# A GNN kernel: nodes laid out by partition in the prologue, small steps moved to ScalarE, and another tail and unread products at the layer borders

## The chip, the cores and the metric

The kernel runs on one core of a Trainium2 chip. The metric is the device time of one execution in microseconds (us), the median of three runs. The core has five engines with queues of their own: TensorE (PE; its weight loads are PEld), VectorE (DVE), ScalarE (ACT), GpSimd (POOL) and SyncE (SP), which here only issues DMAs. The profile comes from one further execution, recorded by the hardware profiler.

## The reference

6250 nodes of 128 features and 200,000 edges (`src`, `dst`), sorted by `dst`. A graph attention layer (GAT) with four heads comes first, then three message passing (MP) layers with batch norm between them, then a final linear map; a residual and a layer norm follow both parts.

```python
xh = (x @ W).reshape(-1, H, C); xi = xh[dst]; xj = xh[src]
alpha = leaky_relu((xi * a_i).sum(-1) + (xj * a_j).sum(-1), 0.2)
...                                   # softmax of alpha over the edges of each dst
x1 = layernorm(x + segment_sum(xj * alpha, dst))
for l in range(3):
    h = emb if l == 0 else (h - mu) * rsqrt(var + EPS) * gamma[l-1] + beta[l-1]
    hk = relu(concat(h[dst], h[src]) @ linA_w[l].T + linA_b[l])
    w = sigmoid(hk @ linB_w[l].T + linB_b[l])
    prop = segment_sum(w * h[src], dst)
    emb = relu(concat(h, prop) @ lin_w[l].T + lin_b[l])
return layernorm(x1 + emb @ final_w.T + final_b)
```

## The kernel before

Edges are worked on in groups of 512 (`GE`), 4 tiles (`T`) of 128 in the partitions: 391 groups in each of four stages, one for GAT and one for each MP layer. A stage first writes a table of one row of 256 floats per node to HBM (`T0`, seen as gat_rows, for GAT; `T1`, mp_rows, for MP). GpSimd's `gather` then fetches the rows of `src` with four indirect DMAs per group into the ring `G` of eight slots, and TensorE, VectorE and ScalarE turn each group into sums for a window of 32 `dst` nodes, added into `acc`. Each engine's program is written out by hand, and semaphores alone order them. GpSimd's first gather of a stage waits until every store of that stage's table has landed.

**Prologue.** `dst` and `src` are loaded as rows of 2048 edges in 98 partitions (`dstI`, `srcI`), 96 full rows first and the tails after; `dst_loaded` counts three DMAs, the last of them issued behind the src rows. SyncE issues these, W0, the two attention columns (`acol`) and the MP weights; ScalarE issues x in five loads. VectorE's instructions up to the index columns are chained by the semaphore `prep` (`then`), and the `PREP_...` numbers say how many must be done: constants, `PREP_REL` (offset of each dst in its window, `relF`), `PREP_REL16` (the same in bf16, `rel16`), `PREP_SRC`, `PREP_MORE` (counts of extra windows), `PREP_IDX`. `edge_columns` on TensorE transposes `relF` and `srcF` with 16 products each, and VectorE copies the result from PSUM to `rel_all` and `idx_all`. GpSimd clears `acc` and `mh` once `PREP_MORE` is reached.

T0 is made in 17 steps `j` of three blocks of 128 nodes. For each, TensorE transposes x (`table_turn`) and multiplies (`table_gat`), ScalarE copies the transposed x (`table_x`), and the result is copied by ScalarE (`table_rows`) or, for j = 6, 7, 9, 10, 12, 13, 15, 16, by VectorE, behind its index columns. SyncE stores each (`store_table`); the ring `tbl` has four slots, so step j waits for the store of step j - 4. The scores of dst (`si_all`, seen as pen) go to `SI` (gat_si) in three stores.

**Border of two layers.** The last group of a layer is followed by steps in which only later stages of the last groups run (`step` with `off >= stop`); `mp_order` gives VectorE's order of stages: `mp_hidden` (pen), `mp_logit` (junk), `mp_C` (selw) and `mp_E` (acc). `mp_agg` on TensorE, for one group, waits for selw of this group and for `mp_E` of the group two before, whose PSUM bank it reuses. Then ScalarE makes the 13 pieces of ReLU (`l_emb`), VectorE the statistics of 25 pieces, and `scaled`, the weights times the new scale. TensorE makes the 25 pairs of table blocks from `scaled`, VectorE adds `constB`, SyncE stores. `extra_windows` handles groups whose nodes span more than one window; each engine reads two numbers from `windows` for it, and skips its body if there are none.

## Time and profile before

| | us |
|---|---|
| median of three runs | 8181.65 |
| lowest, highest | 8179.83, 8184.32 |
| profiled execution, its own time | 8189.58 |
| its span | 8187.5 |
| GpSimd busy | 5969.7 (73%) |
| VectorE busy | 4897.3 (60%) |
| TensorE busy | 4800.6 (59%) |
| ScalarE busy | 1347.8 (16%) |

The span counts from the first to the last recorded instruction. Busy time leaves out the issue of DMAs by SyncE and ScalarE and register work. "Idle before" of a group is the time its engine stood still just before it, with what ended that. A row with a queue's name, such as SPq or ACTq, is an instruction of the engine's sequencer.

### The profile page before, as it was taken

The numbers are of one execution on the slowest core, as the hardware profiler recorded it, in microseconds if no ns is written. First come the engines' busy times: TensorE is split into PE (matmuls) and PEld (weight loads), VectorE is DVE, ScalarE is ACT, GpSimd is POOL, SyncE is SP. The second block draws the span as 40 slices with busy tenths as digits, with TensorE's granted clock in tenths as the row PEclk, the third lists the DMA queues.
The fourth block names the chain that finished last, engine by engine and source line by source line (L and its number), as shares of the span: only waits on it lengthen the run. The fifth ranks groups of instructions, "written<-read, shape, count | busy, mean of one in ns | idle before, by whom it ended". The sixth has DMA issues, their size and how long they took to land.

```text
span 8187.5 us, 133929 instructions
## 1 busy us (share of the span) xinstructions
PE 4800.6 (59%) x26657; PEld 4100.9 (50%) x26658; DVE 4897.3 (60%) x25933; ACT 1347.8 (16%) x5213; POOL 5969.7 (73%) x6318
## 2 busy tenths in 40 slices
PE   5888888888744444445564444445446544444545
PEld 5777777777544444444454444444445444444444
DVE  6778778777655555555565555555555555555555
ACT  2333333333300000000020000000011000000002
POOL 5777777777477777777757777777766777777775
PEclk6555555555655555555565555555556555555555
DMA  5444444444444444444454444444435444444443
GB/s 155 131 134 131 131 131 132 132 131 124 135 129 131 129 129 129 131 129 129 129 155 129 131 129 129 129 131 129 129 113 170 129 131 129 129 129 131 129 129 104
DMA packets 613022, 1074.04 MB, mean 131 GB/s; under 512 B 305928, under 2 KB 371368, under 8 KB 612428
## 3 DMA queue, kind: packets, MB, share of 16 engines
q0 software_dynamic: 300288, 820.39, 34.9%
q1 hardware_dynamic: 306076, 247.79, 10.3%
q10 hardware_dynamic: 6356, 3.20, 0.2%
q14 instruction: 279, 2.29, 0.1%
q8 instruction: 23, 0.38, 0.0%
HBM read 1025.37 MB, written 45.47 MB: 131 GB/s over the span
## 4 chain that ended last, share of the span: by engine, by line
POOL 46%; issue 22%; PE 14%; DMA 7%; DVE 7%; DVEq 2%; POOLq 1%; ACT 1%; ACTq 0%
POOL G L740 46%; DMA G<-mp_rows,idx 5%; PE ps L1717 5%; PE ps L1817 3%; DMA G<-gat_rows,idx 2%; PE ps L1679 2%; DVE junk L1509 2%; PE ps L1714 1%; PE ps L1706 1%; DVEq L1117 1%; PE ps L1769 0%; PE ps L1770 0%; DVE selw L1518 0%; POOLq L737 0%; POOLq L736 0%
## 5 line engine op out<-in xcount | busy, mean ns | idle before, releaser
L740 POOL DMA_INDIRECT G<-mp_rows,idx x4692 | 4439.0, 946 | 1564.2 <-issue 1384.5
L1817 PE MATMUL ps<-selw,G 128*128 128x32 f32 x9384 | 2216.7, 400 | 587.6 <-DVE selw L1518 579.3
L1817 PEld LDWEIGHTS ps<-selw,G 128*128 128x128 f32 x9384 | 2088.9, 328 | 868.9 <-issue 760.0
L1498 DVE TENSOR_TENSOR pen<-ps,G 128x512 f32<-128x512 f32 x1173 | 811.3, 692 | 2730.1 <-DMA G<-mp_rows,idx 2726.9
L1807 PE MATMUL ps<-awin,ring 96*128 96x128 bf16 x4692 | 713.4, 307 | 2315.5 <-DVE ring L1483 2312.4
L740 POOL DMA_INDIRECT G<-gat_rows,idx x1564 | 1489.7, 952 | 497.9 <-issue 442.6
L1807 PEld LDWEIGHTS ps<-awin,ring 96*128 96x128 bf16 x4692 | 408.9, 132 | 2467.4 <-DVE ring L1483 2463.4
L963 ACT ACTIVATE gate<-logit,params 128x4 f32<-128x4 f32 x1173 | 348.6, 297 | 5327.0 <-DVE junk L1509 5205.2
L1509 DVE SCALAR_TENSOR_TENSOR junk<-pen,ps 128x128 f32<-128x128 f32 x4692 | 1056.3, 278 | 0.1
L1483 DVE TENSOR_TENSOR ring<-ring,ps 96x512 bf16<-96x512 bf16 x1173 | 793.3, 676 | 37.1 <-DMA ring<-rel_dst 37.1
L1717 PE MATMUL ps<-sel,weighted 128*128 128x32 f32 x3128 | 748.9, 404 | 0.0
L1717 PEld LDWEIGHTS ps<-sel,weighted 128*128 128x128 f32 x3128 | 696.2, 327 | 25.2
L1679 PE MATMUL ps<-ident,G 128*128 128x128 f32 x1564 | 428.0, 429 | 171.9 <-DMA G<-gat_rows,idx 170.7
L851 ACT ACTIVATE pen<-ring,negbig 128x512 f32<-128x512 bf16 x391 | 282.1, 721 | 1165.8 <-DVE ring L1129 1157.0
L1155 DVE CUSTOM_DVE_ANT_0 junk<-ps,pen 128x512 f32<-128x512 f32 x391 | 268.2, 686 | 264.6 <-issue 257.2
L1679 PEld LDWEIGHTS ps<-ident,G 128*128 128x128 f32 x1564 | 280.1, 217 | 186.7 <-issue 129.2
L1509 DVE DVE_READ_ACCUMULATOR junk<-pen,ps 128x1 f32 x4692 | 369.4, 79 | 0.0
L1706 PE MATMUL ps<-sel,ex 128*4 128x32 f32 x3128 | 230.4, 238 | 199.2 <-DVE tt L1280 199.2
L1488 DVE TENSOR_TENSOR ps<-ps,rel_all 128x128 f32<-128x128 f32 x1173 | 333.0, 284 | 0.0
L1518 DVE TENSOR_TENSOR selw<-ps,gate 128x128 f32<-128x128 f32 x1173 | 331.1, 282 | 0.2
L1706 PEld LDWEIGHTS ps<-sel,ex 128*4 128x4 f32 x3128 | 161.6, 105 | 330.4 <-issue 245.2
L833 ACT COPY idx<-idx_all 128x4 int32 (+1 forms) x1568 | 283.5, 182 | 23.4 <-issue 11.3
(202 smaller groups left out, 4682.6 us busy)
## 6 DMA issues: line engine op xcount, KB each, us to landing
ring<-rel_dst SPq DMA_DIRECT2D x294, 384.0 KB
G<-mp_rows,idx POOLq DMA_INDIRECT x4692
ring<-rel_dst SPq DMA_DIRECT2D x98, 512.0 KB
awin<-mp_dst_rows SPq DMA_DIRECT2D x1173, 24.0 KB
G<-gat_rows,idx POOLq DMA_INDIRECT x1564
mp_rows<-acc SPq DMA_DIRECT2D x36, 512.0 KB, 3.0
mp_dst_rows<-acc SPq DMA_DIRECT2D x36, 384.0 KB, 5.0
sm<-gat_si SPq DMA_DIRECT2D x391, 0.5 KB
```

The source lines that it names most:

```text
L740: pool.indirect_dma_start(out=G[:, u, width * t:width * (t + 1)], out_offset=None, in_=table, in_offset=bass.IndirectOffsetOnAxis(ap=idx[: ...
L963: nc.scalar.activation(gate[:, off % 4, :], logit[:, off % 4, :], ACT.Sigmoid, bias=params[:, l, C_BB:C_BB + 1]).then_inc(done["gate"], 1)
L1483: v.tensor_tensor(selT16[0:S * W, off % 4, :], relbc16[0:S * W, off % U, :], nodeP[0:S * W, :].to_broadcast([S * W, GE]), ALU.is_equal).th ...
L1488: v.tensor_tensor(selP[:, off % 4, :].rearrange("p (t n) -> p t n", t=T), iotaP.unsqueeze(1).to_broadcast([P, T, W]), rel4, ALU.is_equal). ...
L1498: v.tensor_tensor(pen[:, off % 2, :].rearrange("p (t c) -> p t c", t=T), PS[off % 2][:, :].rearrange("p (t c) -> p t c", t=T), Grows[:, of ...
L1509: v.scalar_tensor_tensor(junk[:, P * t:P * t + P], pen[:, off % 2, P * t:P * t + P], 0.0, wP, ALU.max, ALU.mult, accum_out=logit[:, off % ...
L1518: v.tensor_tensor(selw[:, off % 4, :].rearrange("p (t n) -> p t n", t=T), one.rearrange("p (t n) -> p t n", t=T), gate[:, off % 4, :].unsq ...
L1679: i = tr(PS[off % 2][:, P * t:P * t + P], Grows[:, off % U, t, D:2 * D], ident[:, :])
L1706: i = mm(PS[4 + b][0:H, 2 * W:3 * W], ex4[:, b, H * t:H * t + H], sel[:, off % U, W * t:W * t + W], start=(t == 0), stop=(t == T - 1))
L1717: i = mm(PS[4 + b][:, 0:W], R[:, b, D * t:D * t + D], sel[:, off % U, W * t:W * t + W], start=(t == 0), stop=(t == T - 1))
L1807: i = mm(PS[off % 2][:, D * t:D * t + D], selT16[0:S * W, off % 4, P * t:P * t + P], awin[:, off % 4, :], start=True, stop=True)
L1817: i = mm(PS[2 + off % 2][:, 0:W], Grows[:, off % U, t, 0:D], selw[:, off % 4, W * t:W * t + W], start=(t == 0), stop=(t == T - 1))
```

## The change

1. Prologue, layout: blocks of the first 48 hold the nodes 48p + b in partition p instead of 128b + p (`by_partition`). x is loaded, and T0 and SI are stored, with that order in mind, so that a partition's nodes stand together in HBM: a load of x has 128 pieces of 5 KB where it had 1280 of 512 bytes, a store of T0 128 pieces of 3 KB where it had 384 of 1 KB, a store of SI 128 pieces of 384 bytes where it had 2304 of 16. The rows of T0 stand where they stood.
2. W0 and the attention columns are issued before dst and src. VectorE makes all its constants before it waits for them.
3. `rel16` is made by ScalarE, as a plain cast, after table step 3, and waits there for `PREP_REL`; the copy that wraps `idx_all` around is ScalarE's too.
4. Four table stores (`REL_AT`) instead of three stand before the stores of the offsets, and SI is stored at steps 8, 16 and 17.
5. VectorE reads the numbers for `extra_windows` ahead of each stage's loop instead of behind it.
6. Tail of an MP layer: VectorE's order in the last steps is `mp_last`.
7. Ahead of the table of layers 1 and 2, TensorE makes eight products of 512 columns into a PSUM bank that nothing reads.

VectorE in the prologue, from the dst offsets to the first table copies. Here xT holds the two lists and relF, and ring is the table's ring. Before:

```order
L1062 TENSOR_TENSOR xT<-xT,baseF 98x2048
L1065 TENSOR_SCALAR G<-xT 98x4x128x4
L1069 CAST xT<-xT 98x2048
L1073 SCALAR_TENSOR_TENSOR xT<-xT 2x704
L1074 TENSOR_REDUCE moreF<-xT 98x4
L1075 TENSOR_TENSOR moreF<-moreF,baseF 98x4
L1076 TENSOR_SCALAR moreI<-moreF 98x4
L1077 TENSOR_SCALAR moreI<-moreI 98x4
L1083 COPY rel_all<-ps 128x4x98 x4
L1083 CAST idx_all<-ps 128x4x98 x4
L1085 COPY idx_all<-idx_all 128x16
```

and after:

```order
L1076 TENSOR_TENSOR xT<-xT,baseF 98x2048
L1080 CAST xT<-xT 98x2048
L1084 SCALAR_TENSOR_TENSOR xT<-xT 2x704
L1085 TENSOR_REDUCE moreF<-xT 98x4
L1086 TENSOR_TENSOR moreF<-moreF,baseF 98x4
L1087 TENSOR_SCALAR moreI<-moreF 98x4
L1088 TENSOR_SCALAR moreI<-moreI 98x4
L1094 COPY rel_all<-ps 128x4x98 x4
L1094 CAST idx_all<-ps 128x4x98 x4
L1102 COPY ring<-ps 128x3x128
```

The step that writes G (rel16) and the copy from idx_all to idx_all are gone; the rest stands as it stood.

ScalarE in the prologue, from the end of table step 3 to step 6 (G is rel16 here, pen the scores). Before:

```order
L811 COPY ring<-ps 128x384
L817 COPY ring<-ps 128x3x128
L819 COPY ring<-ps 128x3x128
L820 COPY pen<-ps 128x12
L811 COPY ring<-ps 128x384
L817 COPY ring<-ps 128x3x128
L819 COPY ring<-ps 128x3x128
L820 COPY pen<-ps 128x12
L811 COPY ring<-ps 128x384
L817 COPY ring<-ps 128x3x128
```

and after:

```order
L819 COPY ring<-ps 128x384
L825 COPY ring<-ps 128x3x128
L827 COPY ring<-ps 128x3x128
L828 COPY pen<-ps 128x12
L840 CAST G<-xT 98x4x128x4
L819 COPY ring<-ps 128x384
L825 COPY ring<-ps 128x3x128
L827 COPY ring<-ps 128x3x128
L828 COPY pen<-ps 128x12
L819 COPY ring<-ps 128x384
L825 COPY ring<-ps 128x3x128
```

The cast stands behind step 3's copies and ahead of everything that ScalarE does for steps 4 and 5.

VectorE at the end of layer 0, in its last steps (ps is PSUM, pen and junk the hidden values and logits). Before:

```order
L1498 TENSOR_TENSOR pen<-ps,G 128x512
L1529 ISA
L1529 TENSOR_TENSOR acc<-acc,ps 128x32
L1509 SCALAR_TENSOR_TENSOR junk,logit<-pen,ps 128x128 x4
L1518 TENSOR_TENSOR selw<-ps,gate 128x128
L1529 ISA
L1529 TENSOR_TENSOR acc<-acc,ps 128x32
L1518 TENSOR_TENSOR selw<-ps,gate 128x128
L1529 ISA
L1529 TENSOR_TENSOR acc<-acc,ps 128x32
L1529 ISA
L1529 TENSOR_TENSOR acc<-acc,ps 128x32
```

and after:

```order
L1530 TENSOR_TENSOR selw<-ps,gate 128x128
L1509 REGISTER_ALU
L1510 TENSOR_TENSOR pen<-ps,G 128x512
L1521 SCALAR_TENSOR_TENSOR junk,logit<-pen,ps 128x128 x4
L1541 ISA
L1541 TENSOR_TENSOR acc<-acc,ps 128x32
L1530 TENSOR_TENSOR selw<-ps,gate 128x128
L1541 ISA
L1541 TENSOR_TENSOR acc<-acc,ps 128x32
L1541 ISA
L1541 TENSOR_TENSOR acc<-acc,ps 128x32
L1541 ISA
```

The weights (selw) of the last but one group moved ahead of the last group's pen, the first addition to acc moved behind its logits; behind the last of the four additions stood two loads from windows, which now stand ahead of the loop.

The diff, cut to its core:

```diff
@@ prologue, SyncE @@
+            sp.dma_start(rhs0[:, 0:D], W0).then_inc(w0_loaded, 16)
+            with nc.allow_non_contiguous_dma(reason="columns of small weights"):
+                for ij, lo in ((0, C), (1, 0)):
+                    sp.dma_start(acol[:, ij:ij + 1], ...).then_inc(w0_loaded, 16)
             for tile, lst, loaded in edges:
                 sp.dma_start(tile[0:QS, :], ...).then_inc(loaded, 16)
-                if lst is dst:
-                    sp.dma_start(rhs0[:, 0:D], W0).then_inc(w0_loaded, 16)
...
+        def by_partition(table, lo, n):
+            return table[0:NF * NB, :].rearrange("(p b) c -> p b c", b=NF)[:, lo:lo + n, :]
...
-                sp.dma_start(T0[lo * NB:(lo + n) * NB, :].rearrange("(b n) c -> n b c", n=NB),
-                             tbl[:, j % 4, 0:n, :]).then_inc(tbl_out[j % 4], 16)
+                if lo < NF:
+                    to = by_partition(T0, lo, n)
+                else:
+                    to = T0[lo * NB:(lo + n) * NB, :].rearrange("(b n) c -> n b c", n=NB)
+                sp.dma_start(to, tbl[:, j % 4, 0:n, :]).then_inc(tbl_out[j % 4], 16)
...
-            for j in range(3):
+            for j in range(REL_AT):
                 store_table(j)
...
-            sp.wait_ge(prep, PREP_REL16)
+            sp.wait_ge(rel16_made, 1)
@@ prologue, ScalarE @@
-                act.dma_start(xall[0:NB, lo:hi, :], x[lo * NB:hi * NB, :]
-                              .rearrange("(b p) c -> p b c", p=NB)).then_inc(x_in[n], 16)
+                act.dma_start(xall[:, lo:hi, :], by_partition(x, lo, hi - lo)).then_inc(x_in[n], 16)
...
+                if j == REL_AT:
+                    act.wait_ge(prep, PREP_REL)
+                    nc.scalar.copy(rel16..., relF...).then_inc(rel16_made, 1)
...
+            nc.scalar.copy(idx_all[:, NG * T:(NG + LOOKAHEAD) * T], idx_all[:, 0:LOOKAHEAD * T]).then_inc(idx_around, 1)
@@ layers, VectorE @@
                 km = kl + windows_before(dve, l)
+                counts = windows_before(dve, l + 1), windows_before(dve, 1)
...
+                mp_last = ((2, mp_C), (1, mp_hidden), (1, mp_logit), (4, mp_E))
+
                 def step(k0, off, stop=U):
-                    for lag, stage in mp_order:
+                    for lag, stage in mp_order if off < stop else mp_last:
@@ layers, TensorE @@
                 if l > 0:
+                    pe.wait_ge(l_emb, NEM * (l - 1) + 4)
+                    for n in range(8):
+                        mm(PS[5][:, :], ident[:, :], params[:, 0, C_LP:C_LP + 4 * D], start=True, stop=True)
                     pe.wait_ge(l_w, 2 * l - 1)
```

## Rows read from the trace of the kernel before

**Rows 1.** Page, costliest groups: busy us, mean ns of one | idle before, releaser.

```profile
L740 POOL DMA_INDIRECT G<-mp_rows,idx x4692 | 4439.0, 946 | 1564.2 <-issue 1384.5
```

**Rows 2.** GpSimd's waits, whole span: us in total, times, longest us.

```profile
POOL G L740 <- DMA mp_rows<-acc: 135.5, 3, 50.1
```

**Rows 3.** Chain of waits, 0 to 100 us: start us, us, what.

```profile
14.53 5.17 ACTq L797
23.45 0.28 ACT WT L804
...
59.28 7.10 DMA gat_rows<-ring
...
67.27 2.32 DMA gat_rows<-ring
...
70.48 1.10 POOL G L740
```

**Rows 4.** Timeline, all engines, 0 to 60 us: start us, us, engine, line.

```profile
0.79 0.40 SPq L530 DMA_DIRECT2D xT<-in_dst  x1
...
12.66 0.23 DVE L1038 TENSOR_SCALAR ablk<-dhc,acol 128x4 f32<-128x4 f32 x1 [9.46 <-DMA acol<-in_L_gnn_att]
...
15.71 1.23 DVE L1057 CAST xT<-xT 98x2048 f32<-98x2048 int32 x1
...
22.03 5.37 DVE L1065 TENSOR_SCALAR G<-xT 98x2048 bf16<-98x2048 f32 x1
...
31.81 0.27 ACT L820 COPY pen<-ps 128x12 f32<-128x12 f32 x1
...
32.54 3.47 DVE L1083 COPY rel_all<-ps 128x392 f32<-128x392 f32 x4
...
32.63 10.78 POOL L730 MEMSET acc<- 128x12800 f32 x1 [29.58 <-DVE moreI L1077]
...
36.92 3.45 DVE L1083 CAST idx_all<-ps 128x392 int32<-128x392 f32 x4 [0.91 <-PE ps L1644]
...
40.41 8.40 DVE L1085 COPY idx_all<-idx_all 128x16 int32<-128x16 int32 x1
...
43.34 5.44 POOL L731 MEMSET mh<- 128x6400 f32 x1
...
48.84 0.56 DVE L1092 COPY ring<-ps 128x384 f32<-128x384 f32 x1
```

**Rows 5.** DMA issues, 0 to 100 us: KB each, median us to landing.

```profile
gat_rows<-ring SPq DMA_DIRECT2D x16, 384.0 KB, 3.5
...
gat_si<-pen SPq DMA_DIRECT2D x2, 36.0 KB, 7.7
```

**Rows 6.** DMA queues, 10 to 11 us (q1 SyncE, q10 ScalarE): packets, MB, share.

```profile
q1 hardware_dynamic: 44, 0.22, 97.7%
q10 hardware_dynamic: 43, 0.02, 13.7%
```

**Rows 7.** DMA packets in sum, 2 to 15 us.

```profile
DMA packets 3429, 3.18 MB, mean 245 GB/s; under 512 B 345, under 2 KB 3244, under 8 KB 3246
```

**Rows 8.** Timeline, border of layers 0 and 1, 4116 to 4133 us.

```profile
4116.14 3.59 PE L1817 MATMUL ps<-selw,G 128*128 128x32 f32 x16 [1.61 <-DVE acc L1529]
...
4120.19 7.73 ACT L991 ACTIVATE mh<-acc,params 128x500 f32<-128x500 f32 x13 [4.07 <-DVE acc L1529]
4121.73 8.10 DVE L1568 BATCH_NORM_STATS2 stats<-mh 128x6 f32<-128x250 f32 x25 [1.68 <-ACT mh L991]
...
4131.97 1.22 PE L1769 MATMUL ps<-scaled,mh 128*128 128x256 f32 x2 [12.23 <-DVE scaled L1441]
```

**Rows 9.** Stretches there: us, each engine's busy (x), TensorE clock, DMA share, GB/s.

```profile
4131.90:4137.60 5.70, 5.63 (x17) 4.90 (x18) 2.09 (x10) 0.00 (x0) 0.00 (x0) 0.50 0.00 0
4137.60:4158.00 20.40, 20.40 (x97) 17.97 (x96) 16.14 (x24) 0.00 (x0) 0.00 (x0) 0.99 0.83 280
```

**Rows 10.** One line (windows_before), VectorE's queue: ns min/median/max.

```profile
L499 DVEq TENSOR_LOAD <-windows x12: 297/309/328, 2057.1 to 8132.7; - x12
```

More of the change, by code:

```diff
@@ L43 @@
 PREP_IDENT = 3
-PREP_ABLK = PREP_IDENT + 6
-PREP_CONST = PREP_ABLK + 13
-PREP_REL = PREP_CONST + 5
-PREP_REL16 = PREP_REL + 1
-PREP_SRC = PREP_REL16 + 1
+PREP_CONST = PREP_IDENT + 17
+PREP_ABLK = PREP_CONST + 2
+PREP_REL = PREP_ABLK + 5
+PREP_SRC = PREP_REL + 1
 PREP_MORE = PREP_SRC + 5
-PREP_IDX = PREP_MORE + 2 * T + 1
+PREP_IDX = PREP_MORE + 2 * T
 def reached(k0, off, n, done=None):
@@ L119, in gnn_kernel @@
     TO = D + 2 * H
-    SIB = (6, 12, NTB)
+    SIB = (8, 16, NTB)
+    REL_AT, SRC_AT = 4, 7
     TW = 2 * D
@@ L501, in extra_windows @@
         @contextmanager
-        def extra_windows(eng, q):
-            before = windows_before(eng, q)
-            total = windows_before(eng, 1)
+        def extra_windows(eng, q, counts=None):
+            before, total = counts or (windows_before(eng, q), windows_before(eng, 1))
             with eng.If(total > 0):
@@ L530, in _ @@
                 sp.dma_start(tile[0:QS, :], lst[0:QS * QW].rearrange("(q e) -> q e", e=QW)).then_inc(loaded, 16)
-                if lst is dst:
-                    sp.dma_start(rhs0[:, 0:D], W0).then_inc(w0_loaded, 16)
-                    with nc.allow_non_contiguous_dma(reason="columns of small weights"):
-                        for ij, lo in ((0, C), (1, 0)):
-                            sp.dma_start(acol[:, ij:ij + 1], att[0, :, lo:lo + C].rearrange(
-                                "h (c o) -> h c o", o=1)).then_inc(w0_loaded, 16)
             sp.wait_ge(pads_filled, 3)
@@ L829, in _ @@
                     table_rows(j - 1)
+                if j == REL_AT:
+                    act.wait_ge(prep, PREP_REL)
+                    nc.scalar.copy(rel16.rearrange("q (c t p) -> q c p t", c=CQ, t=T),
+                                   relF.rearrange("q (c p t) -> q c p t", c=CQ, t=T)).then_inc(rel16_made, 1)
             def copy_idx(k0, off):
@@ L1036, in _ @@
             then(v.memset(epsc[:, :], EPS))
-            dve.wait_ge(w0_loaded, 48)
-            then(v.tensor_scalar(ablk[:, 0:H], dhc[:, :], acol[:, 0:1], None, ALU.mult))
-            then(v.tensor_scalar(ablk[:, H:2 * H], dhc[:, :], acol[:, 1:2], None, ALU.mult))
-            assert done[0] == PREP_ABLK
             then(v.memset(negbig[:, :], -BIG))
@@ L1054, in _ @@
             assert done[0] == PREP_CONST
+            dve.wait_ge(w0_loaded, 48)
+            then(v.tensor_scalar(ablk[:, 0:H], dhc[:, :], acol[:, 0:1], None, ALU.mult))
+            then(v.tensor_scalar(ablk[:, H:2 * H], dhc[:, :], acol[:, 1:2], None, ALU.mult))
+            assert done[0] == PREP_ABLK
             dve.wait_ge(dst_loaded, 48)
@@ L1064, in _ @@
             assert done[0] == PREP_REL
-            then(v.tensor_single_scalar(rel16.rearrange("q (c t p) -> q c p t", c=CQ, t=T),
-                                        relF.rearrange("q (c p t) -> q c p t", c=CQ, t=T), NONE16, ALU.min))
-            assert done[0] == PREP_REL16
             dve.wait_ge(src_loaded, 48)
@@ L1084, in _ @@
                                        PS[4 + t][:, :].rearrange("p (c q) -> p c q", c=CQ)[:, :, 0:QP]))
-            then(v.tensor_copy(idx_all[:, NG * T:(NG + LOOKAHEAD) * T], idx_all[:, 0:LOOKAHEAD * T]))
             assert done[0] == PREP_IDX
@@ L1302, in _ @@
             dve.wait_ge(acc_cleared, 2)
+            counts = windows_before(dve, 0), windows_before(dve, 1)
             load_bases(0, 0, U)
@@ L1338, in added @@
                 dve.wait_ge(x_scan, scan[0])
-            total = windows_before(dve, 1)
+            total = counts[1]
             with dve.If(total > 0):
@@ L1353, in _ @@
             dve.sem_inc(x_free, 1)
-            with extra_windows(dve, 0) as at:
+            with extra_windows(dve, 0, counts) as at:
                 now, k0 = one_by_one(gat_sems, at.w), GR + at.n
@@ L1553, in _ @@
                 dve.sem_inc(x_free, 1)
-                with extra_windows(dve, l + 1) as at:
+                with extra_windows(dve, l + 1, counts) as at:
                     now, k0 = one_by_one(mp_sems, at.w), GR + at.n
@@ L1657, in _ @@
                 table_gat(j - 1)
-                if j in (4, 7):
-                    edge_columns((4, 7).index(j))
+                if j in (REL_AT, SRC_AT):
+                    edge_columns((REL_AT, SRC_AT).index(j))
             pe.wait_ge(wraw_loaded, 48)
```

17 lines of the change are left out of this document (12 added, 5 removed).

## The prediction, made before the changed kernel was run

> **What bounds the kernel now.** I began with the page's costliest groups: GpSimd issues the indirect gathers, 0.95 us each with 0.3 us of issue between them [rows 1], one every 1.25 us. There are 6256 (four for each of 391 groups, in four stages), so 6256 x 1.25 = 7820 of 8187.5 us is this pace, and the change leaves its instructions alone. What can move is the time in which GpSimd has no gather to issue: the prologue, 70.48 us to the first gather [rows 3], and the borders between stages, three waits for the table of the next layer, 135.5 us in all, 50 for each of the last two [rows 2]. So the views to read are the chain of waits and the timeline of the prologue, the DMA view there, and the timeline and clock of one border.
>
> In the prologue the chain [rows 3] runs: ScalarE issues the loads of x and is stuck in that until 22.1 us (the 14.53 piece is the last of five); then, through TensorE and the table copies, to VectorE's index columns, which end at 40.4; then one copy of 16 columns from SBUF to SBUF that lasts 8.4 us, until GpSimd's second memset ends at 48.78 [rows 4]; then tables 6 to 16, in which the last waits until 66.41 for a store; then that last store and the first gather.
>
> **Prologue, step by step.** The new head of the chain is the arrival of the dst list, call it D, since the column work starts from it. In the old profile VectorE reached it at 15.71, just after its constants [rows 4], so it had landed by then. In the new one it lands later. The x loads now are pieces of 5 KB instead of 512 B, and the weights stand first in SyncE's queue. The two queues take turns packet by packet: at 10 to 11 us 44 against 43 packets, although one kind was 8 KB and the other 512 B [rows 6]. So when x's packets are ten times as large, x gets its bytes early and the list late. Per DMA engine SyncE's queue has 24 small weight packets (384 over 16 engines) and then 12 of 8 KB (both lists; the dst tail waits behind the src list), against 40 of x. By D nearly all of x, 36/40 of 3.2 MB, and 1.6 MB of lists and weights have passed: 4.5 MB. The old start moved 245 GB/s between 2 and 15 us [rows 7], a border with large pieces 280 [rows 9]: D = 2 + 4.5/0.245 = 20.4 or 2 + 4.5/0.28 = 18.1. I take 18.5, since the pieces are large, with 15.7 (what the old order reached) and 20.4 as bounds.
>
> The DMA page of the Trainium skill (DMA: Bandwidth & Descriptors, Queues, rings and completion order) says that an engine drains a whole packet, typically 9 to 17 descriptors, of one queue before it switches. Taken as turns of so many x pieces, all of x would pass ahead of the weights and the lists come last, D = 2 + 4.8/0.28 = 19.1, 0.6 us more; the counts of 44 and 43 speak for turns of one piece.
>
> From D, all on VectorE [rows 4]: cast, minimum, base and difference, 22.03 - 15.71 = 6.32. The bf16 step of 5.37 goes to ScalarE. Then src cast, pads, maximum and counts, 32.54 - 27.4 = 5.1. Then four copies for rel_all, 3.47, and four for idx_all, 3.45. The copy of 16 columns goes to ScalarE. Sum D + 18.35 = 36.9 against 48.84: 11.9 us. Of this, 5.37 + 8.43 + about 0.9 of waiting for TensorE is removed, and 2.8 is given back by the later D.
>
> What runs beside: the weights land at about 10 (24 packets per engine in turns with x of 0.24 us, 2 + 7, and the completion), against 12.66 [rows 4], and ScalarE, whose seven x issues should now cost about 0.4 us each like SyncE's of 96 pieces [rows 4], is free by then. Tables 0 to 3 took 8.6 us from the weight copy at 23.45 [rows 3] to 32.08 [rows 4], so they end near 19. Then ScalarE waits for the differences at D + 6.3 = 24.8 and casts. Behind this wait stand its copies for tables 4, 5 and 6, and TensorE, which waits for the same event. The cast isn't in the trace. Bounds: four times ScalarE's 0.59 for 500 columns [rows 8], 2.4, and VectorE's 5.37 with the same scattered write. I take 2.4. TensorE then is at the src columns at 24.8 + 2.4 + three tables of 1.3 = 31, when VectorE has just made the first rel_all copy (30.8). So the cast is covered by the src half of VectorE's work; at 5.37 about 0.2 us shows, and without cover 3.
>
> Tables 6 to 16: from 48.84 table 12 was stored at 59.28 [rows 3], 10.4 later, and then the store took 7.1, since it queued with a store of gat_si in pieces of 16 bytes (7.7 us to landing, against 3.5 for table rows [rows 5]). Those pieces are now 384 bytes. Table 16 can be copied at 10.4 + 3.5 = 13.9, ends 0.86 later, lands 2.3 later [rows 3], and the gather starts 0.86 after: 18.0, with the store's own issue 18.3, against 70.48 - 48.84 = 21.6. First gather at 36.9 + 18.3 = 55.2: **15.3 us earlier**. Bounds of this part: 2.5 less if TensorE keeps its pace (it idles 2 us now, not 10), 2 more if the copies run slower beside the memset, which now ends near 46. rel_all's copies ran beside it at 0.87 us for 392 columns, against 0.56 for 384 afterwards [rows 4].
>
> **Borders.** The eight unread products start when four of the 13 ReLU pieces are done, 4120.19 + 4 x 0.59 = 4122.6 [rows 8]. TensorE was idle until 4131.97 and then worked 5.7 us at a granted 0.5 (the 1.2 GHz level) before it rose to 0.99 (2.4 GHz) [rows 9]. At the high level the 97 instructions of 20.4 us give 0.21 each, four to a pair of blocks, 0.84; an unread product of 512 columns costs the same, and 1.68 at the low level. With the same 5.7 us at the low level, 3.4 products are done, the other 4.6 take 3.9, end 4132.2. The true products so start 0.2 later but all at the high level, which saves 5.7/2 = 2.85: 2.65 a border, **5.3 us for two**. Behind them are queued only the table's products, and VectorE and the stores follow these (rate 280 GB/s with the clock high, which the stores kept up with). Bounds: 3 above; below, the eight never raise the clock, 8 x 1.68 = 13.4, a loss of 4.1 each.
>
> The tail order: the two last products of a layer took 3.59 together, 1.8 each [rows 8]. The new order lets the weights of the last but one group be made early, but its product also needs its PSUM bank, and that is free only after the addition of two groups before, which the new order puts behind the last group's logits. So not 1.8 but about 0.15 a layer comes out, for the addition of 0.18 that no longer stands ahead of the logits: **0.4 us for three**. Bounds 0 and 5.4.
>
> The register loads: two of 0.31 [rows 10] with their 0.2 of register work, about 1 us, leave the spot between the last addition and the statistics (VectorE's 1.68 idle at 4121.73, of which some 0.6 is ReLU [rows 8]). They stand at the top of the next layer now, where 0.5 us of them shows ahead of the scaling. All of this ends before 4132.2, when the unread products let TensorE go, so I cost it at nothing; without that cover it would be a gain of 0.4 a border.
>
> Sum: 15.3 + 5.3 + 0.4 = 21.0 us. The profiled span of 8187.5 becomes 8166.5, and the median of 8181.65 becomes 8160.6 by the same difference; the run around the profile took 8189.58.
>
> **Rivals.** *Copies locked by the memset.* The 8.4 us copy shows that GpSimd's memset can hold VectorE for its whole length. If the table copies are held as well, table 6 waits for D + 11.4 + 16.15 = 46.1 instead of 36.9: 9.2 us lost, 8169.8. Against it: rel_all's copies, from PSUM too, ran in the same memset [rows 4]. *ScalarE still stuck.* If the loads' issue doesn't shrink, tables 0 to 3 end at 32 as before, the cast at 34.5, the src columns at 38 and the indices at 41.5: 8165.2. Its cause was 1280 pieces a load, against some 128 now. *The clock doesn't rise for unread products:* 5.3 not gained and 2 x 4.1 lost, 8174.1. Against it: the old rise came after the same kind of steady work. *The list comes late.* This is the one that ends slower. x's large packets sit between the list's, and every us of D costs one us, since VectorE has nothing else to do; from D = 18.5 + 21.0 = 39.5 on the whole is slower, 8182 and up. It needs 4.5 MB at 120 GB/s, half of the lowest long mean seen. Up to D = 25 it gives 8167.
>
> **How the numbers follow.** Forecast with its bounds 0.72 (8153 to 8169), locked copies 0.07, stuck issue 0.06, clock 0.07, late list 0.08, of which 0.03 is beyond the point of no gain. Range 8153 to 8173: it leaves out part of the clock case, the late list and the far ends. A measurement of this kernel can tell 0.2%, 16.4 us, that is 8165.3: about four fifths of the forecast lie below it, 0.59. Slower than 8198 needs D near 56; I leave 0.02 for it and what I don't see. Within 0.2%: 0.39.
>
> **What would show it.** The dst cast starts at 17 to 20 and not at 15.7; ScalarE's weight copy at about 10; the cast on ScalarE takes 2 to 3 us; table 6's first copy at 37, right after the index copies; the first gather at 55. At a border, eight products from 4122.6 (shifted), a granted clock near 1 for the whole table, and a wait of GpSimd of 47 instead of 50 us. Wrong would be: D above 21, a long piece among VectorE's copies while GpSimd's memset runs, TensorE not done with the unread products when the scaling is, or another pace than 1.25 us per gather.

## The result, and the profile after

| us | before | after |
|---|---|---|
| median | 8179.64 (15 runs) | 8164.16 (15 runs) |
| lowest, highest | 8176.54, 8184.32 | 8161.66, 8167.09 |
| span of the profiled execution | 8187.5 | 8162.0 |

The ratio is 0.9981, with a 95% interval of 0.9973 to 0.9988: 15.5 us or 0.19% faster, a hair inside the 0.2% that I had named as the limit of what can be told. The forecast was 8160.6 in 8153 to 8173; the sum of 21.0 us was 5.5 too large. The total hides 2 us of that, by luck: the forecast started from 8181.65, the median of three runs, and over 15 runs it is 8179.64.

The two spans differ by 25.5 us, 10 more than the medians: the profiled execution of before took 8189.58 us, more than any of its 15 runs, and that of after 8163.91, close to its median. The starts of GpSimd's first and last gather of each stage divide them:

| piece, us | before | after | difference |
|---|---|---|---|
| start to first gather | 70.48 | 61.20 | -9.3 |
| attention stage, first to last gather | 1964.9 | 1958.0 | -6.9 |
| its last gather to layer 0's first | 120.4 | 120.2 | -0.2 |
| three MP stages, first to last gather | 5864.8 | 5861.9 | -2.9 |
| border of layers 0 and 1 | 50.9 | 48.4 | -2.5 |
| border of layers 1 and 2 | 51.0 | 47.8 | -3.3 |
| last gather to the end | 64.9 | 64.6 | -0.3 |

Without the stages themselves the pieces give 15.6 us, the difference of the medians. What the stages add (9.8 us) is for the most part in the length of the gathers (6.7 and 2.5 us of busy time); these are GpSimd's costliest groups by form (busy us, mean ns of one), of before and of after:

```profile
L740 POOL DMA_INDIRECT G<-gat_rows,idx x1564 | 1489.7, 952 | 497.9 <-issue 442.6 <-DMA gat_rows<-ring 21.7 <-DVE weighted L1265 19.8
```

```profile
L749 POOL DMA_INDIRECT G<-gat_rows,idx x1564 | 1483.0, 948 | 489.3 <-issue 461.3 <-ACT idx L845 14.8 <-DVE weighted L1275 13.1
```

**Prologue.** The timeline of after, 0 to 62 us (start us, us, engine, line, what; in brackets the idle time before it and what ended it), which answers to [rows 4]; the line numbers are higher now:

```profile
0.78 2.77 ACTq L806 DMA_DIRECT2D G<-in_x  x5
...
15.59 0.23 DVE L1066 TENSOR_SCALAR ablk<-dhc,acol 128x4 f32<-128x4 f32 x1 [9.87 <-DMA acol<-in_L_gnn_att]
...
20.23 1.23 DVE L1071 CAST xT<-xT 98x2048 f32<-98x2048 int32 x1 [4.15 <-DMA xT<-in_dst]
...
26.55 9.40 ACT L840 CAST G<-xT 98x2048 bf16<-98x2048 f32 x1 [1.39 <-DVE xT L1076]
...
31.66 3.42 DVE L1094 COPY rel_all<-ps 128x392 f32<-128x392 f32 x4
...
31.75 10.77 POOL L739 MEMSET acc<- 128x12800 f32 x1 [28.70 <-DVE moreI L1088]
...
36.32 1.73 PE L1648 MATMUL ps<-rhs,ring 128*128 128x136 f32 x6 [6.23 <-ACT ring L819]
...
39.55 2.05 PE L1658 MATMUL ps<-ident,xT 98*128 98x98 f32 x16
...
40.27 3.46 DVE L1094 CAST idx_all<-ps 128x392 int32<-128x392 f32 x4 [5.19 <-PE ps L1658]
...
43.76 0.56 DVE L1102 COPY ring<-ps 128x384 f32<-128x384 f32 x1
...
61.20 1.10 POOL L749 DMA_INDIRECT G<-gat_rows,idx  x1 [13.30 <-ACT idx L845]
```

ScalarE's issue of x no longer blocks it. The cast on ScalarE takes 9.40 us. Behind it stand the copies for table steps 4 to 6; TensorE waits 6.23 us for one of them and reaches the src list at 39.55, and VectorE waits 5.19 us for that. VectorE's work on either side of this wait took what it took before.

How the list comes in, by the stretches of after (us, five engines' busy time, TensorE clock, DMA share, GB/s), then the DMA queues of after (q1 SyncE, q10 ScalarE: packets, MB, share) in the same 18.2 us, and last those in the final 2.2 us of them:

```profile
2.00:20.20 18.20, 4.25 (x19) 4.08 (x20) 3.43 (x20) 3.13 (x7) 0.99 (x2) 1.00 1.01 288
```

```profile
q10 hardware_dynamic: 849, 3.19, 55.7%
q1 hardware_dynamic: 1023, 2.06, 45.4%
```

```profile
DMA packets 454, 0.51 MB, mean 234 GB/s; under 512 B 46, under 2 KB 424, under 8 KB 444
...
q1 hardware_dynamic: 328, 0.40, 84.8%
q10 hardware_dynamic: 126, 0.11, 22.5%
```

At 288 GB/s, 18.2 us are 5.2 MB: all of x (3.2 MB) and 2.06 MB of SyncE's queue. The small packets at the end, on SyncE's queue, are not of a list (those are of 8 KB): what stands behind the lists in that queue are the MP weights. The lists are 1.6 MB and W0 0.07, so 0.4 MB of them had passed by 20.2.

**Border.** The timeline of layers 0 and 1 in after, 4098 to 4143 us, which answers to [rows 8]:

```profile
4102.47 0.19 DVE L1541 TENSOR_TENSOR acc<-acc,ps 128x32 f32 x1 [1.52 <-PE ps L1834]
4102.80 7.73 ACT L1005 ACTIVATE mh<-acc,params 128x500 f32<-128x500 f32 x13 [3.91 <-DVE acc L1541]
4103.55 8.10 DVE L1582 BATCH_NORM_STATS2 stats<-mh 128x6 f32<-128x250 f32 x25 [0.88 <-ACT mh L1005]
...
4105.37 10.08 PE L1781 MATMUL ps<-params,ident 128*128 128x512 f32 x16 [3.03 <-ACT mh L1005]
...
4114.13 0.16 DVE L1449 RECIPROCAL mv<-mv 128x1 f32<-128x1 f32 x1 [1.51 <-issue]
...
4115.29 0.60 PE L1786 MATMUL ps<-scaled,mh 128*128 128x256 f32 x2
...
4142.31 0.94 POOL L749 DMA_INDIRECT G<-mp_rows,idx  x1 [47.50 <-DMA mp_rows<-acc]
```

and the stretches there, which answer to [rows 9]:

```profile
4105.37:4111.40 6.03, 6.03 (x7) 2.52 (x8) 6.03 (x20) 6.01 (x10) 0.00 (x0) 0.51 0.00 0
4111.40:4115.50 4.10, 4.10 (x11) 1.90 (x10) 2.31 (x9) 1.21 (x6) 0.00 (x0) 1.00 0.01 2
4115.50:4135.90 20.40, 20.40 (x100) 18.09 (x99) 15.62 (x26) 0.00 (x0) 0.00 (x0) 1.00 0.72 242
```

The clock rises 6 us after the unread products begin, and the whole table runs at 2.4 GHz.

### The profile page after: what moved, and what is told of

The parts are those of the page before. It is cut to its first block, busy times and chain, and to the rows that moved or that the text cites. A ratio compares the mean times of both kernels' runs of the same rounds, so it can differ in the third digit from the quotient of the medians.

```text
span 8162.0 us, 133990 instructions
## 1 busy us (share of the span) xinstructions
PE 4842.2 (59%) x26689; PEld 4118.1 (50%) x26690; DVE 4894.9 (60%) x25931; ACT 1352.9 (17%) x5215; POOL 5960.5 (73%) x6318
## 4 chain that ended last, share of the span: by engine, by line
POOL 54%; issue 22%; PE 8%; DMA 7%; DVE 6%; DVEq 1%; POOLq 1%; ACT 0%; SPq 0%; ACTq 0%
POOL G L749 54%; DMA G<-mp_rows,idx 5%; PE ps L1834 3%; DMA G<-gat_rows,idx 2%; DVE junk L1521 2%; PE ps L1731 1%; PE ps L1693 1%; DVEq L1127 1%; DVE weighted L1275 0%; PE ps L1786 0%; POOLq L746 0%; PE ps L1787 0%; DVE selw L1530 0%; PE ps L1728 0%; POOLq L745 0%
## 5 line engine op out<-in xcount | busy, mean ns | idle before, releaser
L845 ACT COPY idx<-idx_all 128x4 int32 (+1 forms) x1568 | 283.4, 182 | 23.5 <-issue 11.3
L1216 DVE TENSOR_REDUCE e<-ps 128x32 f32<-128x96 f32 x391 | 100.5, 257 | 299.1 <-PE ps L1709 298.7
L1275 DVE TENSOR_TENSOR weighted<-G,ps 128x512 f32<-128x512 f32 x391 | 268.8, 687 | 0.0
```

The source lines that it names most:

```text
L845: nc.scalar.copy(idx[:, T * (off % U):T * (off % U) + T], idx_all[:, bass.ds(k0 * T + off * T, T)]).then_inc(idx_ready, 1)
```

## Experiments

All but before_again start from the changed kernel. They ran in four sets, each on one chip and with its own runs of the kernel before. In two of the sets (rel16_on_vector, cast_written_in_order, no_unread_products and old_tail_order; before_again, prologue_three_edits and all_edits) the kernel before itself took 10555 and 10389 us, since GpSimd stood still for about 3 us again and again inside the stages, whatever the kernel; so of these the prologue and the pieces of a border are compared, event against event. This wait of GpSimd in before_again (us in total, times, longest us) has no counterpart in the first records, and what caused it is not known:

```profile
POOL G L740 <- remote: 968.2, 348, 3.6
```

### The prologue: the cast

**rel16_on_vector**: VectorE makes the bf16 copy again.

```diff
+            then(v.tensor_single_scalar(rel16.rearrange("q (c t p) -> q c p t", c=CQ, t=T),
+                                        relF.rearrange("q (c p t) -> q c p t", c=CQ, t=T), 255.0, ALU.min))
-                if j == REL_AT:
-                    act.wait_ge(prep, PREP_REL)
-                    nc.scalar.copy(rel16..., relF...).then_inc(rel16_made, 1)
```

> The changed kernel with one step undone: the bf16 copy of the offsets is made by VectorE again, behind the differences, as before. The changed kernel's median is 8164.2, its first gather at 61.2. My theory after seeing its trace: the cast took ScalarE 9.40 us and held TensorE's transposes of the src list behind it, so handing it over brought almost nothing. Then VectorE's own chain sets the end: 20.2 + 6.3 + 5.4 + 5.1 + 3.5 + 3.5 = 44.0 for table step 6 against 43.8, first gather at 61.4, total 8164. Rival (the forecast's sum): moving it was worth 5.4 us, the lateness of table step 6 has another cause (the later arrival of the list alone), and undoing it costs 5.4: table step 6 at 49, first gather at 66.6, total 8169.6.

Its timeline (its median is 10499.6, against 10494.6 to 10499.0 of the other three of its set):

```profile
20.47 1.23 DVE L1068 CAST xT<-xT 98x2048 f32<-98x2048 int32 x1 [4.43 <-DMA xT<-in_dst]
...
26.79 5.58 DVE L1076 TENSOR_SCALAR G<-xT 98x2048 bf16<-98x2048 f32 x1
...
44.42 0.56 DVE L1102 COPY ring<-ps 128x384 f32<-128x384 f32 x1
...
61.60 1.10 POOL L750 DMA_INDIRECT G<-gat_rows,idx  x1 [7.86 <-ACT idx L842]
```

The first gather is at 61.6, 41.1 us after the list; with the cast on ScalarE it is 41.0 in the first record (61.20 - 20.23), and 41.0 and 40.2 in two kernels of this set with the same prologue (no_unread_products, old_tail_order). So handing the cast over brought nothing: the rival's 5.4 us are refuted.

**cast_written_in_order**: the same elements, walked in the order in which they are written.

```diff
-                    nc.scalar.copy(rel16.rearrange("q (c t p) -> q c p t", c=CQ, t=T),
-                                   relF.rearrange("q (c p t) -> q c p t", c=CQ, t=T))
+                    nc.scalar.copy(rel16.rearrange("q (c t p) -> q c t p", c=CQ, t=T),
+                                   relF.rearrange("q (c p t) -> q c t p", c=CQ, t=T))
```

> The changed kernel with ScalarE's cast walking its elements in another order: the same 2048 per partition, written one behind the other in bf16 and read with a stride of 16 bytes, where the changed kernel reads in order and writes with a stride of 256 bytes. Theory: the scattered 2-byte write is what makes 9.40 us; written in order the cast takes 2.4 us (four times 0.59 for 500 columns), it is covered, table step 6 starts 5.1 us earlier at 38.7, the first gather at 56.1, total 8159.1. Rival: the cast is slow for its size or its type or for either stride, it stays above 5 us, and the total stays within 1 us of 8164.

```profile
20.90 1.23 DVE L1071 CAST xT<-xT 98x2048 f32<-98x2048 int32 x1 [4.98 <-DMA xT<-in_dst]
...
27.22 4.01 ACT L840 CAST G<-xT 98x2048 bf16<-98x2048 f32 x1 [2.35 <-DVE xT L1076]
...
35.84 3.43 DVE L1094 CAST idx_all<-ps 128x392 int32<-128x392 f32 x4
...
39.31 0.56 DVE L1102 COPY ring<-ps 128x384 f32<-128x384 f32 x1
...
56.73 1.10 POOL L749 DMA_INDIRECT G<-gat_rows,idx  x1 [8.17 <-ACT idx L845]
```

The cast takes 4.01 us instead of 9.40: the scattered write cost more than half. 2.4 was still too low, but at 4.0 VectorE waits for nothing (no idle time before idx_all), and table step 6 follows the list by 18.4 us instead of 23.5, which is the forecast's own 18.35. This is the 5.1 us that the forecast missed. The totals are 10494.6 against 10499.0 and 10495.9 of the two with the slow cast in that set, too close to show 5 us.

### The prologue: the list and the layout

**dst_list_first**: SyncE issues the 96 rows of dst ahead of W0 and the attention columns, as before. **dst_tail_early**: the last two pieces of dst go ahead of the src rows.

```diff
             for tile, lst, loaded in edges:
                 sp.dma_start(tile[0:QS, :], ...).then_inc(loaded, 16)
-            sp.wait_ge(pads_filled, 3)
-            for tile, lst, loaded in edges:
+                sp.wait_ge(pads_filled, 3)
                 sp.dma_start(tile[QS:QF, :], ...).then_inc(loaded, 16)
```

> The changed kernel with SyncE's order undone: the 96 full rows of dst are issued ahead of W0 and the attention columns, as before. The dst list lands at 20.2 in the changed kernel, 15.7 or earlier before. Theory 1 (the queue's order makes it late: 384 small weight packets go ahead, each taking a turn against a 5 KB packet of x): VectorE starts its dst cast 2 to 4 us earlier, the cast of the differences, table step 6 and the first gather with it, while the weight copy comes later than 16.1. Theory 2 (the forecast's sum of bytes: what counts is all that passes until the last list packet, whatever the order within SyncE's queue, since the dst tail stands behind the src rows anyway): the start stays within 0.6 us of 20.2 and the first gather within 0.6 of the changed kernel's.

> The changed kernel with the two last pieces of dst issued right behind its 96 full rows, ahead of the src rows (behind them in the changed kernel). Theory: the dst cast waits for the tail, which waits for the src rows, six packets of 8 KB per DMA engine in turns with x; without them ahead it starts about 0.75 MB / 250 GB/s = 3 us earlier, at 17.2 instead of 20.2, and the first gather comes 3 us earlier. Rival: the full rows of dst themselves land last, or the wait for the pads holds SyncE: under 1 us.

The dst cast and the first gather, of the one and of the other:

```profile
20.49 1.23 DVE L1072 CAST xT<-xT 98x2048 f32<-98x2048 int32 x1 [2.55 <-DMA xT<-in_dst]
...
61.18 1.10 POOL L750 DMA_INDIRECT G<-gat_rows,idx  x1 [13.03 <-ACT idx L846]
```

```profile
18.16 1.23 DVE L1070 CAST xT<-xT 98x2048 f32<-98x2048 int32 x1 [2.39 <-DMA xT<-in_dst]
...
58.64 1.10 POOL L748 DMA_INDIRECT G<-gat_rows,idx  x1 [12.82 <-ACT idx L844]
```

The place of the weights in the queue changes nothing (20.5 against 20.2; tail_add_first, of the same set and with the changed kernel's prologue, has 20.5 too): what counts is all that passes until the list's last packet. The tail's place does matter: 2.1 us at the list and 2.6 at the gather against the first record, 2.4 and 3.0 against tail_add_first, where 3 was expected. Records with the same prologue put the list at 20.2 to 21.5, so differences under 1 us say nothing. The medians were 8166.65 and 8163.26, both against 8180.72 of before.

**layout_as_before**: x, T0 and SI with the old pieces (part 1 of the change undone; SI is still stored at steps 8, 16 and 17, part 4).

> The changed kernel with the node layout of before in the first 48 blocks (x loaded in pieces of 512 bytes, T0 stored in pieces of 1 KB, the scores in pieces of 16 bytes). Theory: ScalarE is stuck in issuing x until about 22 and ends table step 3 at about 32, then casts until 41.5, then copies for table steps 4 to 6: TensorE is at the src list at about 45, VectorE's columns end at 50, and the stores of the scores take 7.7 us instead of 3.5: first gather at 70 to 74, total 8173 to 8177. The other parts of the change alone would so bring nearly nothing in the prologue. Rival: the layout's share is small, since the cast bounds the prologue: first gather at 63, total 8166.

```profile
0.78 17.76 ACTq L803 DMA_DIRECT2D G<-in_x  x5
...
16.60 1.23 DVE L1069 CAST xT<-xT 98x2048 f32<-98x2048 int32 x1 [6.84 <-DMA xT<-in_dst]
...
50.34 0.56 DVE L1100 COPY ring<-ps 128x384 f32<-128x384 f32 x1
...
79.45 1.10 POOL L746 DMA_INDIRECT G<-gat_rows,idx  x1 [35.19 <-DMA gat_rows<-ring]
```

8184.44 us against 8180.72 of before in the same runs, ratio 1.0006 (0.9996 to 1.0015). The list lands 3.6 us earlier, and the first gather is 18.3 us later than in the changed kernel, 9 later than before: ScalarE is late from the issue, and the 9.40 us follow that. Both expectations were too small. The chain to table step 6 was as expected (50); the rest is behind it, 29.1 us from there to the gather against 17.4 with the new layout and 21.6 before [rows 3, 4]. Its chain of waits there (start us, us, what):

```profile
53.63 7.96 DMA gat_rows<-ring
...
68.51 10.05 DMA gat_rows<-ring
```

The last store of the table lands 10.05 us after its issue where before it took 2.32 [rows 3]. That is 7.7 us, the whole of 29.1 - 21.6. It is issued right behind the store of SI of step 16, which before stood at step 12, and of the 4032 packets from 68 to 79 us 3392 are under 512 bytes. So the loss comes from the old 16-byte pieces together with the new places of SI's stores, and this experiment prices the layout in that company, not by itself. Without the new layout the other prologue parts, with the 9.40 us cast among them, lose.

### The borders

**no_unread_products** leaves out the loop of eight products; **old_tail_order** uses `mp_order` in the last steps too.

> The changed kernel without the eight unread products ahead of the tables of layers 1 and 2. Theory: the table then starts with 5.7 us at the low clock and GpSimd's wait at each border grows by 2.65 to 3 us: 50.2 and 50.0 instead of 47.5 and 46.8, total 8169.5 to 8170. Rival: the gain at the borders came from the tail order and the moved register loads, and the products bring under 1 us each: total within 2 us of 8164.

> The changed kernel with the order of VectorE's stages in a layer's last steps as before. Theory: 0.15 to 0.2 us a layer, so from a layer's last gather to its last addition 9.0 us instead of 8.8, total 8164.7. Rival: what the order aims at, 1.8 us a layer, total 8169.6.

GpSimd's waits (us in total, times, longest us), of the one and of the other:

```profile
POOL G L749 <- DMA mp_rows<-acc: 147.2, 3, 57.5
```

```profile
POOL G L749 <- DMA mp_rows<-acc: 141.7, 3, 54.9
```

From the first true product to the next gather it takes 29.7 and 30.6 us without the unread products, 27.1 and 27.1 with them (here, and in the first record of after: 27.0 and 27.1). So they bring 2.6 and 3.5 us, 3.0 on average, where 2.85 was forecast. From the start of the last gather to the end of a layer's last addition the old order takes 16.4, 13.0 and 16.5 us, the new one 16.6, 13.1 and 16.5 in cast_written_in_order: nothing of 1.8 us, as expected, and no gain of 0.15 to 0.2 either. (The 13 to 17 instead of 9 us belong to this set.)

**tail_add_first**:

```diff
-                mp_last = ((2, mp_C), (1, mp_hidden), (1, mp_logit), (4, mp_E))
+                mp_last = ((4, mp_E), (2, mp_C), (1, mp_hidden), (1, mp_logit))
```

> The changed kernel with another order of VectorE's last steps in a layer: the addition of four groups before stands first, then the weights, hidden values and logits. Theory (the forecast's): the early weights of the last group but one gain nothing in the changed kernel since its product also waits for its PSUM bank, which the addition placed behind the last logits frees. With the addition first, that product starts 2.8 us earlier (at about 4095.9 instead of 4098.72), one of the two products that follow the last logits is gone, and a layer's last addition comes 1.5 to 1.7 us earlier: 7.2 us behind the last gather instead of 8.8, 4.8 us in all. Rival: the products wait for something else (the gate of the last group, the rows), and the last addition stays within 0.2 us.

Measured from the last gather, the last addition ends at 7.70, 7.68 and 7.85 us in the three layers, against 8.80, 8.75 and 8.92: 1.1 us a layer, not 1.6. The bank was what the early weights waited for; the weights of the last group remain. Of 3.3 us the median shows some 2 (8162.94 against 8180.72 of before: 17.8 us, where the changed kernel had 15.5; the intervals of the two ratios overlap, so the medians alone don't show it), in part since the border of layers 1 and 2 gained only 0.4: there the unread products ended 0.9 us after the scaled weights were ready. They took 8.5 to 10.2 us in the records, as the clock rose sooner or later in them.

### The kernel before once more

**before_again** is the kernel before, with nothing changed.

> The kernel before, unchanged, recorded once more. In its first record the stage of the attention layer took 1964.9 us from first to last gather, 6.9 more than in the record of the changed kernel, with 132 gathers of over 966 ns where the changed kernel and three variants of it had 66 to 69. Theory 1: that is chance of the one record (the medians differ by 15.5 us, and prologue and borders alone give 9.3 + 6.0): this record has some 67 long gathers, a stage of 1958 to 1960 us at 946 ns a gather (1964 at 949), and again 70.5 us to the first gather and borders of 50.9 and 51.0. Theory 2: the change also made this stage faster: again about 130 long gathers and 5 us more at the same length of a gather.

It had 7 long gathers and not 67 or 130, in a set where gathers are held anyway: neither theory gave that (the variants of the changed kernel had 42 to 59 in the sets with held gathers). The prologue repeats (list at 15.83, the copy of 16 columns 8.45 us, first gather 71.1).

### Edits together

**prologue_three_edits**: the cast in order, the dst tail early, and

```diff
             for n in range(BU):
                 lo, hi = n * NT, min((n + 1) * NT, NF)
+                if n == 2:
+                    act.wait_ge(dst_loaded, 48)
                 act.dma_start(xall[:, lo:hi, :], by_partition(x, lo, hi - lo)).then_inc(x_in[n], 16)
```

**all_edits** adds at the borders tail_add_first, `l_emb` + 1 and `range(7)` for the unread products, and VectorE's reads of `windows` behind the table. **all_edits_cast_behind** also puts the cast at `SRC_AT` instead of `REL_AT`, and SyncE's store of rel16 behind table store 6.

> The changed kernel with three edits in the prologue: ScalarE's cast written in order (4.0 us instead of 9.4 in an earlier run), the tail of dst ahead of the src rows (2.3 us earlier in another), and ScalarE issues the last three of its five loads of x only once the dst list has landed. Theory: the list is late because 5.2 MB pass before it at 288 GB/s; with 1.9 MB of x held back it lands at about 2 + (5.2 - 1.9 - 0.75) / 0.288 = 11 us, table step 6 follows 18.4 us later unless ScalarE's tables 0 to 3 and its cast are now last (they would put it at about 31), and the first gather comes 17.4 later, at 48 to 49: 12.5 us earlier than 61.2, total 8151.5. Rival 1: the held loads of x come back as a wait of table steps 6 and later, 21 us or more after they are issued: first gather at 54, total 8157. Rival 2: the list's own 8 KB packets bound its landing, D stays above 16: first gather at 53 or later.

> The three edits of the prologue together with three at the borders: the addition first in VectorE's last steps of a layer (1.1 us a layer in an earlier run), the register loads behind the table instead of ahead of the scaling, and seven unread products that start after the first ReLU piece instead of eight after the fourth. Theory: the scaled weights are ready 1.1 + 1.2 us earlier, at 18.7 us behind the last gather instead of 21.0 and 20.6, and the unread products have ended by then, since they start 1.8 us earlier against the ReLU: next gather at 45.8 instead of 48.4 and 47.8, and 1.1 at the end of the last layer, so 5.7 us less than the prologue's edits alone: 8146. Rival: with the earlier start the clock falls again before the table or rises no earlier, and the table starts at the low clock: at least one border no better than 47.8.

> The six edits together, and ScalarE's cast now behind its copies for table steps 4 to 6 instead of ahead of them, with SyncE's store of its result behind those tables' stores. Theory: in the run before, TensorE could not start on the src list until 29.59 (behind the cast of 4.1 us and the copies it held up), while VectorE had been ready at 26.4; with the cast behind, the index columns follow rel_all's copies at 26.4, table step 6 starts at 29.9 instead of 33.8 and the first gather at 47.3 instead of 51.2. Against the changed kernel's median of 8164.2 that is 61.2 - 47.3 = 13.9 in the prologue, 2 x 2.3 at the borders and 1.1 at the end: 8144 to 8145. Rival 1: the cast is then in the way of the copies for steps 8 and later: first gather at 51 again, total 8148. Rival 2: TensorE's table steps 4 to 6 wait for stores or x pieces: gather above 52, total over 8149.

The list is there at 11.46 in prologue_three_edits, as the sum of bytes gives, and a wait of VectorE for TensorE takes a part of it back (5.58 us before idx_all), as in all_edits (3.93). Its first gather at 54.0 is the number of rival 1, but not by that mechanism: ScalarE, which waits for the list itself before it issues the last loads, is held in that until 12.7 and makes its weight copy only at 15.15, though TensorE had the product for it at 7.9. The first row below shows the same in the last kernel. Its prologue:

```profile
0.78 12.17 ACTq L807 DMA_DIRECT2D G<-in_x  x5
...
11.72 1.23 DVE L1072 CAST xT<-xT 98x2048 f32<-98x2048 int32 x1 [3.20 <-DMA xT<-in_dst]
...
29.10 3.49 DVE L1095 CAST idx_all<-ps 128x392 int32<-128x392 f32 x4 [1.84 <-PE ps L1658]
...
50.04 1.10 POOL L748 DMA_INDIRECT G<-gat_rows,idx  x1 [10.65 <-ACT idx L846]
```

| us | first gather | border 0/1 | border 1/2 | median | before, same set | ratio |
|---|---|---|---|---|---|---|
| changed kernel | 61.2 | 48.4 | 47.8 | 8164.16 | 8179.64 | 0.9981 (0.9973 to 0.9988) |
| prologue_three_edits | 54.0 | 58.9 | 58.7 | 10303.2 | 10389.16 | 0.9915 (0.9900 to 0.9930) |
| all_edits | 51.2 | 54.2 | 54.2 | 10302.9 | 10389.16 | 0.9916 (0.9903 to 0.9930) |
| all_edits_cast_behind | 50.0 | 47.9 | 45.9 | 8172.24 | 8203.18 | 0.9963 (0.9949 to 0.9976) |

The borders of prologue_three_edits and all_edits belong to the set with held gathers and are not to be held against 48.4 and 47.8. The last is 30.9 us faster than before, twice what the change brought. Beyond the changed kernel its pieces give 11.2 us in the prologue, 0.2 up to layer 0, 0.6 and 1.9 at the borders and 1.1 at the end, 14.9 in all; 30.9 - 15.5 is 15.4. That is 4 to 5 us short of the 19.6 that I expected: the first gather came 2.7 us late, since table step 3 ended at 24.3 and VectorE still waited 1.84 us for TensorE, and the last addition of layer 0 came 9.6 us behind the last gather where that of layer 1 came 7.7 behind it. In the set with 10389 us the change and the three edits took 86 us off the median, most of it in the attention stage (2927 us from first to last gather against 3001 in before_again), and in the set with 10555 us every variant was 55 to 60 us faster than before. The cause of that stays open.

## Why the prediction was right or wrong

**What bounds it.** The pace of 1.25 us per gather stood, and all that the change brought lies in the prologue and the borders.

**The list, D.** 18.5 forecast, 20.2 measured, within its bound of 20.4. It cost 1.7 us. The step that was off is the count of bytes: 4.5 MB, and 5.2 passed. All of x had passed, 3.2 MB where I counted 36/40 of it, and so had 0.4 MB of the MP weights, which stand behind the lists in the queue; the rate of 280 was right (288). dst_list_first and dst_tail_early bear the reading of D as bytes out.

The Trainium skill (DMA: Bandwidth & Descriptors, Queues, rings and completion order), taken as in the prediction, would have given 19.1, nearer, but all of x would have passed ahead of the weights and lists. The trace of after doesn't show that: from 10 to 12 us both queues moved as many packets, and x's last packets came beside those of the lists.

```profile
q10 hardware_dynamic: 72, 0.27, 51.8%
q1 hardware_dynamic: 74, 0.25, 48.6%
```

**The weights.** About 10 forecast; VectorE and TensorE had them at 15.6, so the 256 pieces of 4 bytes of the attention columns, beside 5 KB ones, ended much later than I counted. It cost nothing, because table step 3 ended at 25.2, ahead of the 26.55 at which the cast could begin, with 1.4 us to spare where I had thought of 6.

**The cast.** This is the step that failed, a term of the sum that was mis-sized. "Bounds: four times ScalarE's 0.59 for 500 columns, 2.4, and VectorE's 5.37 with the same scattered write. I take 2.4" and "at 5.37 about 0.2 us shows": it took 9.40, outside both bounds. One engine's time for a scattered write is no upper bound for another's, and I took the end that belonged to a contiguous copy. The path was right (the cast stands ahead of TensorE's src columns), its length was not. In the chain it showed 5.2 us (VectorE's wait), and rel16_on_vector shows the consequence: the removal of 5.37 us that the sum booked was worth nothing. The 0.2 us at 5.37 were also too little by the forecast's own terms: 24.8 + 5.37 + 3.9 is 34.1, and the index copies were due at 33.4, so 0.7 shows. In order it took 4.01, and the forecast's 18.35 from list to table step 6 came out at 18.4.

**VectorE's chain.** 6.32, 5.1, 3.47 and 3.45 forecast; 6.3, 5.1, 3.42 and 3.46 measured. The wrap copy's 8.4 us are gone; ScalarE's took 0.23 us at 56.0, when no memset ran any more.

**Tables 6 to 16.** 18.3 forecast, 17.4 measured. With the two misses: 15.3 - 1.7 - 5.1 + 0.9 = 9.4, measured 9.3. The 0.9 lies inside the bounds of 2.5 less and 2 more.

**Borders.** 2.65 each forecast and 0.15 for each tail, 5.6 for two; measured, tails included, 2.5 and 3.3, 5.8 for two. The high clock gave 3.0 (the forecast 2.85). The true products started 0.7 and 0 us later against the last addition than before (forecast 0.2).

**Register loads.** At nothing: right in the sum, for a reason that I had half. The statistics began 0.8 us earlier, but the scaling then waited 1.51 us where it had waited 0.36 before: the three loads at the layer's top are 1.2 us, not 0.5, on the way to the scaled weights. They cancel to within 0.35.

**Tail order.** 0.15 a layer forecast, 0.19, 0.17 and 0 between the records of before and after, and nothing in old_tail_order: too small to be shown either way. That the early weights wait for a bank, and what the order would bring with the addition first, is shown by tail_add_first, though I had 1.6 us and it gave 1.1.

**Rivals.** Copies locked by the memset: refuted, table step 6's copy took 0.56 us while a memset ran to 47.9. ScalarE stuck: refuted, 2.77 us for five issues. Clock: refuted, in every border with unread products the table took 27.0 to 27.2 us to the next gather, against 29.7 and 30.6 without them. Late list: happened by 1.7 us, far from the 39.5 at which it would have lost. Another rival, that ScalarE is the slower engine for this cast, was not among them; the page of before held no row that excluded it.

**The 10 us between span and median.** In its record the attention stage of before had 132 gathers of over 966 ns and the changed kernel's 66. Whether the kernel before always has them is not settled. Against it speak the 7 of before_again, and layout_as_before: by the pieces outside the stages it should be 2 us slower than before, with 5.7 us saved in that stage 4 us faster, and its median was 3.7 slower.

## What to carry to other kernels

Before a strided elementwise step is handed to another engine, measure it there: the time of one engine is no bound for the other, and the order in which elements are walked (reads scattered, writes in order) can be worth more than the engine. A step that is moved off the critical engine stands in front of what the other engine does next; put it behind what the path still waits for. When a list lands late, count all bytes of all queues up to its last packet, and hold back those that nobody needs yet, but not by a wait in the queue of an engine whose own work stands behind it. A part that is undone in company of the others is priced in that company: the old layout with the new places of SI's stores cost 7.7 us that the old layout did not cost before.

## What the runs showed of the hardware

- ScalarE's cast of 98 x 2048 f32 to bf16 took 9.40 us with 2-byte writes 256 bytes apart and 4.01 with writes in order and reads 16 bytes apart; VectorE took 5.37 to 5.58 for the scattered form.
- The copy of 16 columns took VectorE 8.40 and 8.45 us beside GpSimd's memset, and ended with it; ScalarE's took 0.23, with no memset beside it. Whether ScalarE's would be as short beside one, no run shows.
- A store of 256 KB of table rows took 10.05 us to land right behind a store in pieces of 16 bytes (layout_as_before), and 2.32 without one just ahead [rows 3].
- Eight products of 512 columns took 8.5 to 10.2 us from case to case, as the clock rose sooner or later in them. A pause of up to 1.6 us behind them (all_edits, seven products) did not bring it down: from the first true product to the next gather it still took 27.1 us.
- A gather takes 946 ns in the median of one execution and 949 in another, whatever the kernel. Over 6256 of them that is 19 us, more than the whole change:

```profile
L749 POOL DMA_INDIRECT G<-mp_rows,idx x4692: 942/946/1459, 2139.4 to 8097.5; - x196
```

```profile
L748 POOL DMA_INDIRECT G<-mp_rows,idx x4692: 942/949/1465, 2134.0 to 8105.5; - x196
```

The first is the changed kernel's (ns min/median/max, first and last start in us), the second that of all_edits_cast_behind. So spans of single records say little here, and pieces between events, or medians of runs made together, say more.
